# Local attention: the clip by a reduction over pairs, and the token shift's split moved from VectorE to ScalarE and GpSimd

## The reference

```python
def shift_token(t):                       # second half of the features comes from the token before
    t1, t2 = jnp.split(t, 2, axis=-1)
    t2 = jnp.pad(t2, ((0, 0), (1, 0), (0, 0)))[:, :-1]
    return jnp.concatenate([t1, t2], axis=-1)
def l2norm(t):
    return t / jnp.clip(jnp.linalg.norm(t, axis=-1, keepdims=True), 1e-12)

h = shift_token(x)
q, k, v = jnp.split(h @ wqkv, 3, axis=-1)       # 8 heads of 64
q = l2norm(q) * qs;  k = l2norm(k) * ksc
q, k = rotary_xpos(q, k)
o = local_attention(q, k, v)                    # windows of 64, each looks at itself and the one before
x = x + o @ wo
```

## Time and profile before

| what | us |
|---|---|
| median of 3 runs | 1533.08 |
| the profiled execution | 1545.77 |
| its span, first to last instruction | 1544.0 |
| attention of the first of the two layers, about | 757 to 1052 |
| attention of the second, about | 1151 to 1440 |

### The profile page before, as it was taken

The page is one execution under the profiler, slowest core; times in us unless marked ns, Lnnn a source line. Parts: engine busy times, 40 slices in busy tenths (PEclk is TensorE's granted clock), DMA queues, the critical chain, the costliest instruction groups (busy, mean ns, idle before and its releaser), DMA issues. The chain is left out here.

```text
span 1544.0 us, 26296 instructions
## 1 busy us (share of the span) xinstructions
PE 1237.7 (80%) x7828; PEld 800.8 (52%) x7828; DVE 1138.3 (74%) x2560; ACT 865.4 (56%) x2259; POOL 829.3 (54%) x760
## 2 busy tenths in 40 slices
PE   6889999854228988479689988885877998898797
PEld 3333333353116877334257666663555766666465
DVE  1299999847118877356589999982658999999464
ACT  5623333243114544237578878783746887888664
POOL 0064344245750555541177767676746776777663
PEclk9999999967559999869889999997998999999999
DMA  3700000031120122130100000000000000000001
GB/s 113 251 1 0 1 0 1 0 104 44 49 90 1 42 63 65 47 120 1 50 1 3 2 1 1 0 1 1 1 22 1 2 2 2 1 1 1 1 1 55
DMA packets 35031, 44.06 MB, mean 29 GB/s; under 512 B 5621, under 2 KB 24978, under 8 KB 34913
## 3 DMA queue, kind: packets, MB, share of 16 engines
q1 hardware_dynamic: 30304, 34.27, 7.0%
q0 software_dynamic: 4608, 8.47, 1.7%
HBM read 22.65 MB, written 21.12 MB: 28 GB/s over the span
## 5 line engine op out<-in xcount | busy, mean ns | idle before, releaser
L1865 ACT ACTIVATE W<-W,nm 128x128 f32<-128x128 f32 x512 | 197.9, 393 | 0.0
L1648 POOL TENSOR_TENSOR W<-W,rden 128x512 f32<-128x512 f32 x128 | 133.0, 1040 | 117.7 <-DVE rden L1966 111.5
L1633 POOL TENSOR_TENSOR R<-R 128x512 f32<-128x512 f32 x128 | 162.6, 1292 | 34.8 <-DVE R L1936 34.8
L1936 DVE TENSOR_TENSOR R<-bank,tab 128x1024 f32<-128x1024 f32 x128 | 151.0, 1214 | 17.0 <-ACT sq L1831 13.1
L1959 DVE CUSTOM_DVE_ANT_0 W<-bank,mask_q,rn 128x128 f32<-128x128 f32 x512 | 146.3, 338 | 7.7 <-issue 4.2
L1194 POOL DMA_INDIRECT expert_rows<-Yt,xin x80 | 83.2, 1040 | 115.4 <-DVE Yt L1167 89.1
L1849 ACT ACTIVATE QK<-bank 128x512 f32<-128x512 f32 x128 | 75.5, 590 | 68.0 <-PE bank L1720 61.1
L616 DVE TENSOR_TENSOR_SCAN S<-beta,U 128x512 f32<-128x512 f32 x64 | 100.0, 1583 | 0.0
L1865 ACT ACTIVATION_READ_ACCUMULATOR W<-W,nm 128x1 f32 x512 | 98.5, 192 | 0.0
L1770 PE MATMUL bank<-PT,VA 128*64 128x128 f32 (+1 forms) x1024 | 86.3, 262 | 13.9 <-issue 10.9
L1745 PE MATMUL bank<-QK 64*64 64x128 f32 x2048 | 85.8, 282 | 11.6 <-DVE nm L1959 11.3
(11 more groups left out here) (310 smaller groups left out, 3583.3 us busy)
## 6 DMA issues: line engine op xcount, KB each, us to landing
expert_slots<-empty SPq DMA_DIRECT2D x8, 650.0 KB, 6.4
xin<-expert_slots SPq DMA_DIRECT2D x8, 650.0 KB
expert_rows<-empty SPq DMA_DIRECT2D x8, 512.0 KB, 6.7
pair_rows<-expert_rows SPq DMA_DIRECT2D x16, 256.0 KB, 4.2
expert_raw<-w1e_dram SPq DMA_DIRECT2D x9, 256.0 KB, 2.8
expert_raw<-w2e_dram SPq DMA_DIRECT2D x9, 256.0 KB, 3.0
tok<-x_dram SPq DMA_DIRECT2D x8, 256.0 KB, 4.5
out_dram<-tok_out SPq DMA_DIRECT2D x8, 256.0 KB, 2.7
```

Source lines behind the costliest of these rows:

```text
L1633: nc.gpsimd.tensor_tensor(halves[:, :, 0, :, z, :], halves[:, :, 0, :, z, :], halves[:, :, 1, :, 1 - z, :], ALU.add).then_inc(summed, 1)
L1648: nc.gpsimd.tensor_tensor(x, x, scale.to_broadcast([P, 4, P]), ALU.mult).then_inc(scaled, 1)
L1865: m = nc.scalar.activation(x, x, ACT.Exp, scale=-1.0, bias=nm[:, p % RING, j:j + 1], accum_out=den[:, p % RING, j:j + 1])
L1936: nc.vector.tensor_tensor(R[:, i, qk, :, :].rearrange("p c (h d) -> p c h d", d=DH), x, y.to_broadcast([P, 2, HEADS, DH]), ALU.mult).then_ ...
```

## The change

Three edits, all in `local_layer`.

1. The clip. The sums of squares go into a new tile `sums`, in which a column of the constant 1e-24 stands beside each sum; the maximum of each pair is taken by a second `tensor_reduce` of 128x32 into 128x16. It takes the place of the `tensor_scalar` of 128x16.
2. The high parts of the shift go from DVE to ACT, as copies in tiles 0 and 1 between the first exponentials and `keep_rows`.
3. The low parts go from DVE to POOL, in tiles 0 and 2 between `add_halves` and `scale_keys`. POOL waits for its own additions ahead of each (`summed`), for ACT's high part (`hs_hi`), and behind each for its own result (`shifted`). The semaphores now count two for a chunk. For the first chunk of a layer, both high parts are made by ACT behind its table load, and both low parts by POOL.

```diff
+            sums = k.sb(f"sums{l}", [P, 2, 2 * HEADS, 2], ctx=ctx)
 ... (POOL)
+                def shift_low(g, par, part):
+                    hi, lo = hs[0][par], hs[1][par]
+                    early_rows, late_rows = shifted_views(k, here(g))
+                    wait_alone(k, pool, hs_hi, 2 * (g + l) + part + 1)
+                    if part == 0:
+                        nc.gpsimd.tensor_tensor(lo[0:DH, :], early_rows, hi[0:DH, :].bitcast(F32), ALU.subtract).then_inc(shifted, 1)
+                        wait_alone(k, pool, shifted, 2 * (g + l) + 1)
+                    else:
+                        nc.gpsimd.tensor_tensor(later(lo[DH:P, :]), late_rows, later(hi[DH:P, :]).bitcast(F32),
+                                                ALU.subtract).then_inc(shifted, 1)
+                        wait_alone(k, pool, shifted, 2 * (g + l + 1))
+                shift_low(G0, 0, 0)
+                shift_low(G0, 0, 1)
...
                             add_halves(g, t)
                             if t % 2:
                                 mix_values(g, par, t // 2)
+                            else:
+                                pool.wait_ge(summed, 2 * (NTILE * g + t + 1))
+                                shift_low(g + 1, 1 - par, t // 2)
                             scale_keys(g, par, t)
 ... (PE)
-                            pe.wait_ge(shifted, g + 1 + l)
+                            pe.wait_ge(shifted, 2 * (g + 1 + l))
 ... (ACT)
+                def shift_high(g, par, part):
+                    hi = hs[0][par]
+                    early_rows, late_rows = shifted_views(k, here(g))
+                    if part == 0:
+                        need(act, v_mm, NTILE * (g - 1))
+                        nc.scalar.activation(hi[0:DH, :], early_rows, ACT.Copy).then_inc(hs_hi, 1)
+                    else:
+                        nc.scalar.activation(later(hi[DH:P, :]), late_rows, ACT.Copy).then_inc(hs_hi, 1)
+                shift_high(G0, 0, 0)
+                shift_high(G0, 0, 1)
...
                         if ex:
                             weights(ex[0], ex[2])
+                        if project and t < 2:
+                            shift_high(g + 1, 1 - par, t)
                         if rows:
                             keep_rows(*rows, 1)
 ... (DVE)
+                nc.vector.memset(sums[:, :, :, 1:2], CLIP2)
-                def shift_part(g, par, part):
-                    ...
-                for part in range(4):
-                    shift_part(G0, 0, part)
...
-                    nc.vector.tensor_reduce(ss[:, i, :], sq[:].rearrange("p q (h d) -> p (q h) d", d=DH), AX.X,
-                                            ALU.add).then_inc(sums_r, 1)
+                    nc.vector.tensor_reduce(sums[:, i, :, 0:1].rearrange("p h o -> p (h o)"),
+                                            sq[:].rearrange("p q (h d) -> p (q h) d", d=DH), AX.X, ALU.add).then_inc(sums_r, 1)
                     dve.wait_ge(sums_r, n + 1)
-                    nc.vector.tensor_scalar(ss[:, i, :], ss[:, i, :], CLIP2, None, ALU.max).then_inc(clipped, 1)
+                    nc.vector.tensor_reduce(ss[:, i, :], sums[:, i, :, :], AX.X, ALU.max).then_inc(clipped, 1)
...
                         if project:
-                            shift_part(g + 1, 1 - par, t)
                             rotate(g, t)
```

More of the change, by code:

```diff
@@ L1908, in _ @@
             def _(dve):
+                nc.vector.memset(sums[:, :, :, 1:2], CLIP2)
                 nc.vector.memset(lnb[:], 0.5 * LN_SHIFT * 0.6931471805599453).then_inc(made, 1)
-                def shift_part(g, par, part):
-                    hi, lo = hs[0][par], hs[1][par]
-                    early_rows, late_rows = shifted_views(k, here(g))
-                    if part == 0:
-                        need(dve, v_mm, NTILE * (g - 1))
-                        nc.vector.tensor_scalar(hi[0:DH, :], early_rows, 1.0, None, ALU.mult)
-                    elif part == 1:
-                        nc.vector.tensor_scalar(later(hi[DH:P, :]), late_rows, 1.0, None, ALU.mult).then_inc(hs_hi, 1)
-                    elif part == 2:
-                        dve.wait_ge(hs_hi, g + 1 + l)
-                        nc.vector.tensor_tensor(lo[0:DH, :], early_rows, hi[0:DH, :].bitcast(F32), ALU.subtract)
-                    else:
-                        nc.vector.tensor_tensor(later(lo[DH:P, :]), late_rows, later(hi[DH:P, :]).bitcast(F32),
-                                                ALU.subtract).then_inc(shifted, 1)
-                for part in range(4):
-                    shift_part(G0, 0, part)
                 def rotate(g, t):
```

## The result

On the same chip the kernel before takes 1533.36 us (median of 4 runs, 1531.53 to 1534.69) and the changed kernel 1498.49 us (4 runs, 1496.23 to 1500.83): a ratio of 0.9773, with an interval of 0.9755 to 0.9792. The forecast was 1503. Two more comparisons, made beside the experiments, gave 0.9783 and 0.9769.

What follows compares the result with a forecast made beforehand. DVE, busy 33.72 of a chunk's 33.99 us, was taken as the bound. Chunks 34.8 + second chunks 5.0 - starts 4.6 - clock 5.0 = 30.2 us gained; 1533.1 - 30 = 1503, range 1489 to 1523.

Steps and rivals of the forecast that it cites:

- The bound, and the clip: Attention stage: DVE is full; the clip waits for POOL's running instruction, the reduction does not, relieving DVE of 3.35 us a chunk.
- The sums: Work per attention chunk after the change: DVE 27.4 us, PE 30.2, ACT 29.4, POOL 29.4.
- The chunk: Attention loop: a chunk takes 31.5 us against a mean of 34.4, 2.9 us for each of 12 chunks: 34.8.
- The rival in which PE packs perfectly: Long tiles catch up ACT's lag from short ones; chunk about 30.4 us, total 1490; chance 0.11.
- The slower rival: POOL's 3.10 us wait before the weights stays, so its subtractions add to the chunk in full; total 1565; chance 0.05.
- second rival: POOL becomes the bound: a tile of 8.2 us, a chunk of 33, total 1523; chance 0.13.
- The starts: Start of each layer: PE starts 2.3 us later with nothing to cover it; twice, 4.6 us lost.
- The second chunks: Second chunk of each layer: DVE is full there too; 2.5 us gained each, 5.0 for two layers.
- The clock and the jumps: Behind the loop's jumps: PE's granted clock falls and DVE no longer hides it; 3 x 1.7, 5.0 us lost.
- The sum: Whole kernel: 34.8 + 5.0 - 4.6 - 5.0 = 30.2 us gained.
- The first chunks: First chunk of each layer: no attention runs beside the projection, DVE waits on ACT, and nothing is gained.
- the reduction waits: New reduction waits as the clip did, the first edit does nothing; pace about 32.3 us, total 1515; chance 0.04.

Runs made afterwards that it cites:

- e10: Changed kernel with the output projection computed for only 128 of each 256 tokens, leaving out half its matmul time; ratio 0.9661 to the kernel before.
- e5: Changed kernel with ACT's copies for later chunks cut to 8 columns (16), part of the computation left out; ratio 0.9745 to the kernel before.
- e6: Changed kernel with POOL's subtractions for later chunks cut to 8 columns (16), part of the computation left out; ratio 0.9777 to the kernel before.
- e4: Changed kernel with the first shift of each layer back on DVE, later ones staying with ACT and POOL; ratio 0.9753 to the kernel before.
- e2: Changed kernel with the old tensor_scalar clip put back, so the shift alone is moved; ratio 0.9814 to the kernel before.
- e7: Changed kernel with one more POOL subtraction of 64x512 in each even tile, into a spare tile; ratio 0.9830 to the kernel before.
- e1: Changed kernel with the shift put back on DVE, so the clip alone is changed; ratio 0.9783 to the kernel before.
- e9: Changed kernel with the shift back on DVE, each part behind the rotation, and the clip's reduction kept; ratio 0.9808 to the kernel before.

## Why the prediction was right, and where it was not

**The bound, and the clip.** The mechanism was right: DVE was full, and relieving it moved the time. The clip was to cost 0.16 from start to start and costs 0.10 (911.10, and the next instruction at 911.20); its record is 186 ns. That the reduction would wait like the clip did is refuted by 64 instances.

**The sums.** DVE was forecast at 27.4 and shows 27.87; ACT 29.4, 29.25; PE 30.2, 31.13 by its records, which run on a little. POOL was forecast at 29.4 and shows 27.17, mostly because the figure counted short waits (0.26 ahead of each part, 0.17 ahead of the copies, 0.1 between instructions, 1.6 us in the chunk) as work. The first subtraction took the 1.27 us that was taken from the earlier trace rows, the other part 1.09.

**The chunk.** 31.5 was forecast and 31.63 measured, for the reason given: the long tiles at PE's pace (e10), tile 0 at ACT's (e5), and POOL with room (e6). The rival in which PE packs perfectly put the chunk at 30.4. With ACT's copies cut down, e5 still has 31.29, and PE's records fill 31.09 us of that: by them PE's own work in a short tile is 6.9 to 7.1 us and not 6.6. How much of this is records that run on is not shown.

**The slower rival.** It needed POOL's 3.10 us ahead of the weights to stay. They are gone in even tiles; 41.2 us of such waits became 13.2. (The prediction ties a loss to POOL as the bound and sends the reader to its second rival for the time; that rival is a gain, 1523, and the loss stands in this one.)

**The starts.** 2.3 us each were forecast. PE starts 5.57 us behind the last operation of the feed-forward half in layer 1 and 5.63 in layer 2, where before had 3.4 in both: 2.2 each. e4 shows that this is the shift alone.

**The second chunks.** The term was mis-sized: 2.5 us each forecast, 0.98 and 0.97 measured (31.45 to 30.47, and 31.54 to 30.57). DVE was full there too, but PE now shows this:

```profile
790.00:830.00 40.00, 39.10 (x437) 29.57 (x436) 35.01 (x126) 37.45 (x130) 34.45 (x35) 1.00 0.01 2
```

39.10 us busy of 40 against 36.06. I subtracted from DVE's time without working out PE's sum for this stage.

**The clock and the jumps.** The term was mis-sized. I took 5.0 us off, three times 1.7, since PE's lost clock at a jump would count once DVE no longer hid it. It does count now, but less. In the profiled execution the clock falls behind two of the four jumps (0.78 and 0.59 on average over 4 us) and stays at 1.00 behind the other two; before it fell behind three. From one sum of squares to the next, the first tile behind a jump takes 8.78 us where it fell, and 7.46 (first layer) and 7.79 us (second) where it did not: 1.3 and 1.0 us lost. That is also why one plain chunk of each layer is longer than the others (32.56 and 32.55 us). In before the same tile takes 8.50 us where the clock stayed and 8.50 to 8.69 where it fell, so there DVE did hide it. What the prediction left out is DVE's own stand at a jump. The tile with the jump is longer than the same tile elsewhere by 3.2, 3.2, 1.6 and 1.5 us before and by 1.7, 1.6, 1.9 and 1.9 after. Jumps and clock together cost 9.8 us before and 8.8 after: 1.0 was gained where 5.0 were taken off.

**The sum.** The loop parts gained 18.0 and 14.8, 32.8 us, where 34.8 - 5.0 = 29.8 were forecast. Of these, 31.8 are the plain tiles', 3.0 less than the 34.8 that were forecast for 12 chunks. By the traces, layer 1 lost 18.8 us and layer 2 13.6, the rest of the program behind the start of layer 1 1.2: 33.6 us. The medians differ by 34.9, the forecast was 30. That it came so near is in part luck: the jumps were 6.0 better than forecast, the plain chunks 3.0 and the second chunks 3.1 worse. The first chunks, at which nothing was counted, gained 2.1 and 0.5 in these executions, but scatter by as much in the changed kernel alone (26.2 to 28.4).

**What the prediction did not say.** It spoke of two edits whose relief of DVE is added (3.35 + 3.2), and so the reader would give each of them half of the gain. The experiments say otherwise. Either edit alone takes DVE far enough below PE: with the clip alone DVE is busy for 30.09 of 31.00 us and PE for 30.18, level with each other, and the chunk is at 31.2 to 31.4. The move then adds two prices (0.4 us in tile 0, 2.2 us in each start) and shortens DVE's stands at the first layer's jumps (loop part 192.2 to 185.5). By the loop parts, second chunks and starts that is 6.8 - 1.5 + 1.5 - 4.4 = 2.4 us of gain for the move on top of the clip, and 2.4 to 3.8 by the table: less than the intervals can show (0.9783 against 0.9769 to 0.9783). The rival "the reduction waits" had the same flaw: it put the shift alone at 1515 from 1533, 0.988, and e2 measured 0.9814 with a chunk of 32.04, where the rival said 32.3.

## What to carry to other kernels

A small operation on DVE beside a busy POOL can cost as much as POOL's running instruction; before moving work away, look whether another form of it (a reduction, which kept its 186 ns) does not wait. Two edits that relieve the same engine don't add up: work out the sum of the next engine in every stage, and count for each edit alone what it brings down to that. Work that is free in the steady part can still cost at a start where nothing covers it, and there the old place may be the better one (e4). At a layer's end nothing covers a late engine either: 4.6 of e7's 10.6 us were lost there.

## What the runs showed that I had not expected

DVE stands at the first layer's jumps in all of the kernels read here, and for most of that time no engine is the cause. In e1 it stands 2.55 and 1.95 us, with the shift's part in front; in e9, with the rotation in front, 2.62 and 0.95; in the changed kernel once, 2.66 us ahead of the rotation at 875.09. The view names ACT's squares there, but they began at 872.39 and took 0.58, which leaves 2.1 us. What stands first changes the second stand and not the first. Why is open; that instructions have to be fetched there was not tested.

TensorE's granted clock falls behind some jumps and not behind others, in the same kernel: in the three executions of the changed kernel it fell behind two, one and two of the four jumps. At the first layer's jumps PE stood 1.18 and 1.24 us where the clock then fell, and 1.18 to 1.45 us where it did not. What decides is open.

POOL's subtraction takes 1.27 us on 64x512 and 1.09 on 64x510, where the second has its columns in two runs of 255; the shorter time is far more than two columns are worth, and no experiment was made on it.
